# Closing layer norm of a two-layer transformer kernel: two fused vector operations per token tile in place of one vector and three GpSimd operations

## The reference

```
mu    = mean(h1);  var = mean((h1 - mu)**2)          # per token, over 256 features
ln    = (h1 - mu) / sqrt(var + 1e-5) * ln_g + ln_b
gamma = w @ Wg.T + bg;   beta = w @ Wb.T + bb        # per batch, 256 features each
out   = gamma * ln + beta + h1                       # h1 = attention output + layer-1 input
```

## Time and profile before

| | |
|---|---|
| median of 3 runs | 1471.73 us (1468.3 to 1472.59) |
| profiled execution, its own time | 1463.25 us |
| span of that execution | 1461.4 us |
| mean granted TensorE clock | 0.939 of full speed |
| busy: PE, DVE, ACT, POOL | 1268.9, 857.6, 676.5, 231.6 us |

### The profile page before, as it was taken

One profiled execution on the slowest core, in us unless ns is written; L12 is line 12 of the kernel. 1 busy time (PEld: TensorE's weight loads), 2 busy tenths in 40 slices (PEclk: granted clock), 3 DMA queues, 4 the chain that ended last, 5 costly groups with the idle time before them and its releaser, 6 DMA issues.

```text
span 1461.4 us, 19153 instructions
## 1 busy us (share of the span) xinstructions
PE 1268.9 (87%) x7052; PEld 607.9 (42%) x7052; DVE 857.6 (59%) x1739; ACT 676.5 (46%) x1328; POOL 231.6 (16%) x256
## 2 busy tenths in 40 slices
PE   7586879999889998999899989999899988995871
PEld 5233444445444543454444544354444442442211
DVE  2542367754876468746866478747775577425611
ACT  1053216465456446545546545545546545650360
POOL 3002100210122003300212003200221020202002
PEclk9579889999999999999999999999999999996686
DMA  3503104240514042411524061503323152015002
GB/s 122 163 17 88 44 1 102 47 87 9 133 32 115 2 102 55 102 32 19 137 46 88 1 140 23 126 2 68 88 58 76 16 120 52 2 15 124 1 1 52
DMA packets 57924, 91.61 MB, mean 63 GB/s; under 512 B 10622, under 2 KB 21470, under 8 KB 57830
## 3 DMA queue, kind: packets, MB, share of 16 engines
q1 hardware_dynamic: 56822, 89.57, 27.1%
q10 hardware_dynamic: 1008, 0.81, 0.2%
HBM read 25.46 MB, written 4.77 MB: 21 GB/s over the span
## 4 chain that ended last, share of the span: by engine, by line
PE 59%; DVE 17%; DMA 7%; issue 6%; SPq 5%; ACT 4%; POOL 2%; POOLq 0%; DVEq 0%; ACTq 0%
PE SX L806 11%; PE OP L781 10%; PE DN L863 10%; PE SC L793 10%; DVE MX L623 8%; PE DN L909 8%; PE DN L888 6%; DMA KS<-PART 3%; SPq L383 3%; DMA OC<-OE 2%; DVE STAT L630 2%; PE SX L809 1%; PE DN L876 1%; ACT E L500 1%; DVE XN L670 1%
## 5 line engine op out<-in xcount | busy, mean ns | idle before, releaser
L623 DVE TENSOR_REDUCE MX<-SX 128x1 f32<-128x512 f32 (+3 forms) x1024 | 556.1, 584 | 288.7 <-PE SX L809 197.5
L500 ACT ACTIVATE E<-SC 128x512 f32<-128x512 f32 (+3 forms) x1024 | 469.2, 520 | 370.1 <-PE SC L793 180.8
L806 PE MATMUL SX<-KS,QS 96*128 96x512 bf16 (+3 forms) x1024 | 328.3, 364 | 91.0 <-DVE MX L623 70.2
L793 PE MATMUL SC<-QS,KS 99*128 99x512 bf16 (+3 forms) x1024 | 297.4, 351 | 17.3 <-ACT E L500 9.0
L781 PE MATMUL OP<-E,V 128*32 128x512 f32 (+3 forms) x2048 | 235.4, 531 | 1.1 <-ACT E L500 1.1
L793 PEld LDWEIGHTS SC<-QS,KS 99*128 99x128 bf16 x1024 | 97.2, 98 | 284.2 <-ACT E L500 180.7
L806 PEld LDWEIGHTS SX<-KS,QS 96*128 96x128 bf16 x1024 | 100.0, 99 | 237.9 <-DVE MX L623 162.6
L909 PE MATMUL DN<-XT,W 128*128 128x512 f32 x256 | 123.9, 611 | 2.2 <-ACT HID L542 1.3
L888 PE MATMUL DN<-XT,WQKV 128*128 128x512 f32 x256 | 118.0, 604 | 2.5 <-DVE X L684 1.3
L418 POOL TENSOR_TENSOR RSTD<-VE,HALF 128x4 f32<-128x4 f32 x32 | 32.6, 1018 | 545.5 <-DVE VE L635 545.5
L863 PE MATMUL DN<-W,HID 128*128 128x256 f32 x512 | 117.2, 382 | 0.0
(11 more groups left out here) (89 smaller groups left out, 973.2 us busy)
## 6 DMA issues: line engine op xcount, KB each, us to landing
QS<-PART SPq DMA_DIRECT2D x96, 256.0 KB, 5.2
KS<-PART SPq DMA_DIRECT2D x96, 256.0 KB, 7.8
OC<-OE SPq DMA_DIRECT2D x64, 128.0 KB
RB<-recip_sums SPq DMA_DIRECT2D x64, 128.0 KB, 2.6
XIN<-in_x SPq DMA_DIRECT2D x8, 512.0 KB, 9.8
ROW<-row_vectors SPq DMA_DIRECT2D x8, 512.0 KB, 4.0
out<-OUT SPq DMA_DIRECT2D x8, 512.0 KB, 2.9
W<-in_w SPq DMA_DIRECT2D x2, 1024.0 KB, 12.7
```

The lines of the kernel that those rows point to most:

```text
L500: a.activation(E[:, at["step"].index() % 2, j, lo:T], SC[(4 * s + j) % 3][:, lo:T], ACT.Exp, scale=HD ** -0.5 if attend == 0 else 1.0)\
L623: v.reduce_max(MX[:, qt, h:h + 1], SX[at["scan"].index() % 2][:, 0:w], AX.X, negate=True)\
L793: ins = t_.matmul(SC[u % 3][:, lo:T], KS[attend][0:ALL_ROWS, h, kt * P:kt * P + P], QS[attend][0:ALL_ROWS, h, lo:T], start=True, stop=atte ...
L806: ins = t_.matmul(bank[:, 0:w], QS[layer][0:CUT_ROWS, h, qt * P:qt * P + P], KS[layer][0:CUT_ROWS, h, 0:w], start=True, stop=layer == 1)
```

## The change

`norm_o` becomes `gain1`, and `close1` moves from behind `stat_a` to in front of it. In `gain1` DVE computes `OUT = (TMP - mean) * G`, four scalar_tensor_tensor that don't need `RSTD`, and POOL computes `RH = TMP + S`, one operation over [128, 1024], into the residual's buffer. POOL's instruction stands behind its `RSTD` of `proj1`. In `close1` DVE computes `OUT = OUT * rstd + RH`, four scalar_tensor_tensor. POOL's three operations of `close1` are gone. The store waits for DVE, and the load of `ROW1` waits for both users.

```
-    s s norm_o p s s nm0b a p s s max0b s a s stat_a p a s s p s a s s p s s a s close1 s norm_a p s s a
+    s s gain1 p s s nm0b a p s s max0b s a s close1 stat_a p a s s p s a s s p s s a s s norm_a p s s a
...
 POOL
+                elif what == "gain1":
+                    wait(pool, row1_dma, at["rows1"].at(16))
+                    wait(pool, dense_done, marks["stat"])
+                    g.tensor_tensor(RH[:], TMP[:], ROW1[:, 1:2, :].to_broadcast([P, TT, D]), ALU.add)\
+                        .then_inc(plus_pool, 1)
                 elif what == "close1":
-                    wait(pool, norm_dve, at["norm"].at(4))
-                    wait(pool, row1_dma, at["rows1"].at(16))
-                    g.tensor_tensor(OUT[:], OUT[:], ROW1[:, 0:1, :].to_broadcast([P, TT, D]), ALU.mult)\
-                        .then_inc(close_pool, 1)
-                    g.tensor_tensor(TMP[:], TMP[:], ROW1[:, 1:2, :].to_broadcast([P, TT, D]), ALU.add)\
-                        .then_inc(close_pool, 1)
-                    wait(pool, close_pool, c.at(3, 2))
-                    g.tensor_tensor(OUT[:], OUT[:], TMP[:], ALU.add).then_inc(close_pool, 1)
+                    marks["close"] = at["norm"].at(4, 4)
...
 DVE
+                elif what == "gain1":
+                    wait(dve, row1_dma, at["rows1"].at(16))
+                    wait(dve, store_dma, at["close"].at(16))
+                    for t in range(TT):
+                        v.scalar_tensor_tensor(OUT[:, t, :], TMP[:, t, :], MV[:, t, 0:1], ROW1[:, 0, :],
+                                               ALU.subtract, ALU.mult).then_inc(gain_dve, 1)
+                elif what == "close1":
+                    wait(dve, rstd_pool, at["norm"].at(1, 1))
+                    wait(dve, plus_pool, at["gain"].at())
+                    for t in range(TT):
+                        wait(dve, gain_dve, at["gain"].at(4, t - 3))
+                        v.scalar_tensor_tensor(OUT[:, t, :], OUT[:, t, :], RSTD[:, t:t + 1], RH[:, t, :],
+                                               ALU.mult, ALU.add).then_inc(norm_dve, 1)
...
 SP
                     else:
-                        wait(sp, close_pool, at["close"].at(3))
+                        wait(sp, gain_dve, at["gain"].at(4))
+                        wait(sp, plus_pool, at["gain"].at())
                         sp.dma_start(ROW1[:], ...)
...
                 elif what == "close1":
-                    wait(sp, close_pool, at["close"].at(3, 3))
+                    wait(sp, norm_dve, at["norm"].at(4, 4))
                     sp.dma_start(out[...], OUT[:])
```

More of the change, by code:

```diff
@@ L82 @@
         "scale0": {"scale": 1}, "scale1": {"scale": 1},
-        "keep0": {"keep": 1, "x_in": 1}, "close1": {"close": 1}, "stat_a": {},
+        "keep0": {"keep": 1, "x_in": 1}, "gain1": {"gain": 1}, "close1": {"close": 1, "norm": 1}, "stat_a": {},
         "mods": {}, "rows": {}, "stackq0": {}, "stackq1": {}, "stackk0": {"stack0": 1}, "stackk1": {"stack1": 1}}
@@ L93 @@
     ADDS[f"up_{_n}"] = {"dense": 1}
-for _n in ("norm_m", "norm_1", "norm_a", "norm_o"):
+for _n in ("norm_m", "norm_1", "norm_a"):
     ADDS[_n] = {"norm": 1}
@@ L97 @@
 COUNTS = ("dense", "res", "bias", "maxima", "max0", "max1", "hold", "pack", "sums", "scale", "rows0",
-          "rows1", "keep", "x_in", "close", "stack0", "stack1", "high", "low", "low1", "norm", "head", "step", "group",
+          "rows1", "keep", "x_in", "gain", "close", "stack0", "stack1", "high", "low", "low1", "norm", "head", "step", "group",
           "scan", "halves")
@@ L294, in two_layers @@
         keep_dve = sem("keep_dve")
-        close_pool = sem("close_pool")
+        gain_dve = sem("gain_dve")
+        plus_pool = sem("plus_pool")
         store_dma = sem("store_dma")
@@ L410, in _ @@
             pool.wait_ge(consts, N_CONSTS)
+            marks = {}
             def work(at, kind, what, b):
@@ L415, in work @@
                 if what in ("stat_a", "proj0", "down_3", "proj1"):
+                    marks["stat"] = at["dense"].at(1, 2)
                     wait(pool, stat_dve, at["norm"].at(9, 9))
@@ L455, in work @@
                     wait(pool, dense_done, at["dense"].at())
+                    if "close" in marks:
+                        wait(pool, norm_dve, marks["close"])
                     g.tensor_tensor(RH[:], R1[:], BP1[:].unsqueeze(1).to_broadcast([P, TT, D]), ALU.add)\
                         .then_inc(hold_pool, 1)
-                elif what == "close1":
-                    c = at["close"]
-                    wait(pool, norm_dve, at["norm"].at(4))
-                    wait(pool, row1_dma, at["rows1"].at(16))
-                    g.tensor_tensor(OUT[:], OUT[:], ROW1[:, 0:1, :].to_broadcast([P, TT, D]), ALU.mult)\
-                        .then_inc(close_pool, 1)
-                    g.tensor_tensor(TMP[:], TMP[:], ROW1[:, 1:2, :].to_broadcast([P, TT, D]), ALU.add)\
-                        .then_inc(close_pool, 1)
-                    wait(pool, close_pool, c.at(3, 2))
-                    g.tensor_tensor(OUT[:], OUT[:], TMP[:], ALU.add).then_inc(close_pool, 1)
+                elif what == "gain1":
[3 more added lines that the diff above has]
+                        .then_inc(plus_pool, 1)
+                elif what == "close1":
+                    marks["close"] = at["norm"].at(4, 4)
             run_passes(work)
@@ L658, in work @@
                     stats(at, XIN)
-                elif what in ("norm_a", "norm_m", "norm_1", "norm_o"):
-                    src = {"norm_a": XIN, "norm_m": XR, "norm_1": R1, "norm_o": TMP}[what]
-                    dst = OUT if what == "norm_o" else XN
+                elif what in ("norm_a", "norm_m", "norm_1"):
+                    src = {"norm_a": XIN, "norm_m": XR, "norm_1": R1}[what]
                     wait(dve, rstd_pool, at["norm"].at(1, 1))
[L664 to L668, removed]
+                    wait(dve, dense_full, c.at())
                     for t in range(TT):
-                        v.tensor_scalar(dst[:, t, :], src[:, t, :], MV[:, t, 0:1], RSTD[:, t:t + 1],
+                        v.tensor_scalar(XN[:, t, :], src[:, t, :], MV[:, t, 0:1], RSTD[:, t:t + 1],
                                         ALU.subtract, ALU.mult).then_inc(norm_dve, 1)
+                elif what == "gain1":
[11 more added lines that the diff above has]
+                                               ALU.mult, ALU.add).then_inc(norm_dve, 1)
                 elif what in ("q0", "k0", "q1", "k1"):
@@ L713, in work @@
                     wait(dve, bias_pool, at["bias"].at())
-                    if what == "proj0":
-                        wait(dve, close_pool, at["close"].at(3))
+                    wait(dve, plus_pool, at["gain"].at())
                     if what == "down_1":
```

## The result

The changed kernel takes 1477.01 us (median of 10 runs, 1473.54 to 1481.96), the kernel before 1471.8 (10 runs, 1468.06 to 1475.09). The ratio is 1.0043, with a 95% interval of 1.0029 to 1.0058: slower, by 6.3 us of 1471.8 (4.3 to 8.5). The medians themselves lie 5.2 us apart. The forecast was +5.7.

What follows compares the result with a forecast made beforehand. PE (87% busy) was taken as the bound, with DVE and PE hand over hand in the touched stretch. Terms +9.1 + 8.0 + 1.6 - 9.0 - 4.0 = +5.7 us on 1471.7 gave 1477.4, range 1468.5 to 1481.5.

Steps and rivals of the forecast that it cites:

- The price of an instruction: One 128x256 scalar_tensor_tensor on DVE: 472 ns, lower bound 407; four in a row 1.68 us, 1.6 between other instructions.
- dearer: Rival: waits before closing instructions break their overlap, `close1` costs 2.0 us; sum +9.3, 1481 us; chance 0.18.
- Part 1: `gain1` on DVE held by POOL's add: 1.7 us in passes 3, 4, 7, 1.0 to 1.5 in 2, 5, 6; +9.1 us.
- the add doesn't hold `gain1`: Rival: scalar_tensor_tensor doesn't meet POOL as tensor_tensor does; sum -2.6 us, 1469.1; chance 0.18.
- Part 2: `close1` on DVE before `stat_a`: 5 x 1.6 = +8.0 us in passes 2 to 6, 0 in 7, +1.6 in 8.
- covered: Rival: PE's attention work covers `close1`, so 8.0 us falls away; sum -2.3, 1469.4 us; chance 0.12.
- Part 3: POOL's three closing operations gone, so `norm_a` falls from 3.30 to 1.37 us; 5 x 1.8 = -9.0 us in all.
- Part 4: Tail: `gain1` starts beside `RSTD`, then POOL's add and `close1`; store some 4 us earlier, -4.0 us (2.8 to 4.5).

Runs made afterwards that it cites:

- the kernel with the new tail alone: Kernel before with the new closing (two scalar_tensor_tensor a tile on DVE, one POOL add) for the last batch only: 1466.91 us, ratio 0.9973.
- the two narrow kernels: Changed kernel with `close1` on 8 of 256 columns, alone and with POOL's add also behind `nm0b`: 1466.14 us (0.9966) and 1454.46 us (0.9897).
- twice the `close1`: Changed kernel with four more scalar_tensor_tensor behind `close1`, into a buffer nothing reads: 1491.79 us, ratio 1.0136 to the kernel before.
- the narrow one: Changed kernel with `close1` on 8 of the 256 columns of each tile: 1466.14 us, ratio 0.9966 to the kernel before.
- the late add: Changed kernel with POOL's add moved behind `nm0b`: 1470.7 us, ratio 1.0007; with `close1` on 8 columns as well: 1454.46 us, 0.9897.
- the last experiment: Changed kernel with `close1` on 8 of 256 columns and POOL's add behind `nm0b`: 1454.46 us, ratio 0.9897 to the kernel before.

## Why the prediction was right

The forecast of 1477.4 met 1477.01, the sum of +5.7 met +6.3, and the mechanisms are those that it named. It was not right in every term, and one thing that it left out is in the time. That the total comes so close is in part luck. The sum had +6.4 us for parts 1 to 3 in passes 2 to 6, and the clean passes give some 5.0 (1.15, 1.35, 1.35, 0.5 and 0.7; pass 3 of the kernel before stands in for its pass 4, and the 159.94 of the kernel with the new tail alone, whose loop is the same, for its pass 6). If passes 7 and 8 cost the 3.3 of the sum, which no run weighs by itself, and the tail gives 4.1, the mechanisms alone make some +4.2 by this estimate. The interval of the measured time begins at 4.3, and the rest may be the clock's.

- **The price of an instruction.** 472 ns was taken, 475 to 477 measured; four in a row 1.68 taken, 1.66 measured. So the rival "dearer" (2.0 for the four of `close1`) falls. The estimate by the Trainium skill's "VectorE: DVE Perf Modes", 424 ns, was 11% low for this form.
- **Part 1, the add holds `gain1`.** Forecast 3.0 to 3.3 us for the four, measured 3.05 in each of passes 2 to 7. So the rival "the add doesn't hold `gain1`" falls. Forecast a delay of 1.0 to 1.7 us a pass, of which 0.3 is `gain1`'s own length. The holding alone is thus 1.2 us a pass on average over passes 2 to 6, and it is 1.15 in a clean pass (159.61 - 158.46). The average hit, the split between the passes did not: the forecast had a holding of 1.4 in pass 3 and of 0.7 in pass 5, where the DMA of `KS` was to cover part of it, and the two narrow kernels show 1.20 and 1.15. PE's wait for the split was put at 1.5 us or more, and is 0.96. The Trainium skill's rule, in "SBUF — State Buffer", section "Who interferes with whom" (a VectorE instruction with two SBUF inputs and a GpSimd instruction that reads SBUF exclude each other), holds for scalar_tensor_tensor as well: with the add out of the way the group fell from 3.05 to 1.66 us.
- **Part 2, `close1` on the chain.** Taking 1.02 us out of it (1.66 to 0.64) takes 1.04 out of a clean pass (160.65 - 159.61). In a clean pass it is on the chain in full. The rival "covered" would have shown nothing. In pass 8 it falls between DVE's reductions as forecast, behind the fourth, and the next scan tile of PE waits 1.57 us for DVE, where the earlier trace rows had reductions without a gap:

```profile
1361.40 1.66 DVE L683 SCALAR_TENSOR_TENSOR OUT<-OUT,RSTD,RH 128x256 f32<-128x256 f32 x4
...
1363.73 1.20 PE L819 MATMUL SX<-KS,QS 96*128 96x512 bf16 x2 [1.57 <-DVE MX L627]
```

- **Part 3, `norm_a` comes free.** Forecast 1.8 a pass, measured 1.6 to 1.8 in clean passes and -9.7 us in the whole, against -9.0.
- **Part 4, the tail.** Forecast -4.0, measured -4.1 in the profile and -4.0 in the runs. The detail was otherwise than put down: DVE goes first, its four take 1.67 and are not held, and POOL's two instructions take 0.17 to 0.19 us longer each (1.19 and 2.53 against 1.02 and 2.34).
- **The clean pass.** By the sum a pass as pass 3 should cost 1.7 + 1.6 - 1.8 = +1.5; measured +1.35 (160.66 - 159.31). Pass 5 should cost 1.0 + 1.6 - 1.8 = +0.8; measured +0.5 (160.64 - 160.16).
- **What the sum left out: the clock.** Parts 1 and 2 make PE wait, and behind these waits the granted clock falls in some passes. In pass 3 of the changed kernel PE waits 0.96 us for POOL's split of the maxima, and the transposes after it take 0.58 us where they took 0.38:

```profile
564.66 0.58 PE L935 MATMUL DN<-ID,NMP 128*24 128x128 bf16 x4 [0.96 <-POOL NMP L449]
```

The slices of 5 us of pass 3 (first two) and of pass 4 (last two), the same work a pass apart: in both PE is busy 3.14 of the first 5 us, and the clock falls to 0.50 behind it in one and not in the other. The waits ahead of the fall are the same in both.

```profile
560.27:565.27 5.00, 3.14 (x21) 1.01 (x20) 4.26 (x8) 1.75 (x4) 1.36 (x5) 0.91 0.31 77
565.27:570.27 5.00, 4.95 (x26) 2.00 (x25) 3.76 (x9) 2.52 (x8) 0.00 (x0) 0.50 0.02 5
...
721.97:726.97 5.00, 3.14 (x22) 1.00 (x21) 4.26 (x8) 1.89 (x5) 1.36 (x5) 1.00 0.30 88
726.97:731.97 5.00, 3.94 (x36) 1.44 (x34) 4.77 (x16) 2.59 (x9) 0.00 (x0) 1.00 0.19 67
```

That cost 1.0 us (161.70 - 160.66), although PE was busy 2.5 us longer (151.72 against 149.21). Most of the rest came out of PE's next wait, the one behind `close1` and the statistics. It is 1.63 us in the clean pass 4, but 0.27 in pass 3 and 0.54 in pass 6, where the clock was low ahead of it:

```profile
572.06 0.39 PE L819 MATMUL SX<-KS,QS 96*128 96x512 bf16 x1 [0.27 <-DVE MX L627]
...
732.68 0.39 PE L819 MATMUL SX<-KS,QS 96*128 96x512 bf16 x1 [1.63 <-DVE MX L627]
...
1053.98 0.39 PE L819 MATMUL SX<-KS,QS 96*128 96x512 bf16 x1 [0.54 <-DVE MX L627]
```

So a slow PE and a late DVE overlap in part, and what a fall costs depends on the waits behind it: 1.0 us in pass 3 and next to nothing in pass 6. The clock would explain why the experiments that change PE's waits moved the whole by more than their direct cost, and one by less: twice the `close1` 13.7 for 9.6, the narrow one 11.3 for some 7.1 (7 x 1.02), the late add 10.1 for 7.8 where `close1` was narrow and 5.3 where it was not. Of these gaps only the first two are clear of the noise, and barely. The mean granted clock of all runs points the same way: 0.930 to 0.931 for the changed kernel, the late add and the doubled `close1`, 0.934 for the kernel before, 0.940 for the last experiment. How these microseconds divide between the passes of one kernel was read from single profiles, and why one pass falls and its twin doesn't stays open. The kernel before has such falls too, in its passes 4 (161.00 at 0.99) and 6, from about 23 us into the pass on, behind the held `norm_a`, where the changed kernel has none. So part of the change's own +6.3 may be the clock's. Least is known of passes 7 and 8: the changed kernel took 152.06 us for pass 7 (clock 0.91), and the one with twice the `close1` 147.59 (0.95).

## What to carry to other kernels

Look for such meetings in the kernel as it is (a group whose mean lies far above that of a group with the same work), for moving one entry of the order can be worth more than a rewrite. And use a new form only where its latency is the time, here in the tail, and keep the old one where its work is hidden.

## What the runs showed of the hardware

- Who comes first matters. `gain1` behind POOL's add lost 1.39 us (3.05 against 1.66). In the tail, where VectorE's short instructions are there first, VectorE lost nothing (1.67 for the four), and POOL lost 0.17 in `RSTD` and 0.19 in the add, which met only the last of the four. I had put down 0.3 for the first and a wait to the end of `gain1` for the second.
- A scalar_tensor_tensor on 8 columns is far from 32 times shorter than one on 256: four take 0.64 us, against 1.66.
- The clock can fall in one pass and not in the next with the same waits to 0.01 us ahead of it (0.76 and 0.96 us of PE in passes 3 and 4). The fall cost 1.0 us in pass 3 and less than 0.1 in pass 6, because a later wait for VectorE shrank from 1.63 to 0.27 and 0.54 us.
- The instructions that wait for met semaphores in front of each `close1` instruction cost nothing: 1.66 us for four, as `gain1` takes without them.
